# A transformer attention stage in double periods: scores of four units in one burst, two weighted sums back to back

## The reference, cut to what matters

```
x = x + L0_attn(L0_cond(x, cond), W_qkv, W_out)     # 16 heads of 64, causal
   qkv    = inputs @ W_qkv
   score  = einsum('bihd,bjhd->bijh', q, k) / 8, masked to j <= i
   w      = softmax(score, axis=2)
   out    = einsum('bijh,bjhd->bihd', w, v) @ W_out
h = L0_cond2(x)                                     # gates f, i, h:
   f, i   = sigmoid(x @ W_f + b_f), sigmoid(x @ W_i + b_i)
   f_n,i_n= f / (f + i + eps), i / (f + i + eps)
   hidden = scans over the positions of f_n and i_n * (x @ W_h + b_h)
x = x + L0_ffn(h) ; x = x + L1_attn(...) ; x = x + L1_ffn(...)
```

## Time and profile before

| | |
|---|---|
| Median of 3 runs | 1017.2 us (1015.59 to 1017.58) |
| Profiled execution, its span | 1016.5 us |
| PE busy | 977.0 us (96%) |
| PE weight loads busy | 789.2 us (78%) |
| DVE busy | 876.8 us (86%) |
| ACT busy | 831.3 us (82%) |
| POOL busy | 471.2 us (46%) |
| Scores of the first attention (L341) | first at 15.4 us, last at 422.0 us |

### The profile page before, as it was taken

How to read it: one execution, slowest core, us unless ns; L and a number is a source line. 1 busy time by engine, 2 the same in 40 slices (tenths; PEclk the granted TensorE clock), 3 DMA queues, 4 the chain that set the end, 5 groups by cost and what they waited for, 6 DMA issues and landing times.

```text
span 1016.5 us, 25956 instructions
## 1 busy us (share of the span) xinstructions
PE 977.0 (96%) x8939; PEld 789.2 (78%) x8939; DVE 876.8 (86%) x3718; ACT 831.3 (82%) x2232; POOL 471.2 (46%) x541
## 2 busy tenths in 40 slices
PE   7999999999999999999989999999999999999897
PEld 6898888888888989743268988888777777776566
DVE  6777989898989888799998899889988888896985
ACT  6888888888888888887797878776887888886786
POOL 2334545454545463606810112102887888893041
PEclk9999999999999999999999999999999999999999
DMA  9000000000000000000000000000000000000002
GB/s 376 35 2 2 2 2 2 2 2 2 2 2 2 2 2 2 2 1 0 1 1 1 1 1 1 1 11 11 23 23 23 23 23 23 23 3 1 1 2 84
DMA packets 8723, 18.31 MB, mean 18 GB/s; under 512 B 1296, under 2 KB 5648, under 8 KB 8208
## 3 DMA queue, kind: packets, MB, share of 16 engines
q1 hardware_dynamic: 8592, 16.65, 4.9%
HBM read 10.36 MB, written 2.10 MB: 12 GB/s over the span
## 4 chain that ended last, share of the span: by engine, by line
PE 79%; DVE 9%; ACT 6%; POOL 3%; issue 3%; DMA 0%; DVEq 0%; ACTq 0%; POOLq 0%
PE PB L245 8%; PE PB L246 8%; PE PB L247 8%; PE PB L341 6%; PE PB L396 6%; PE PB L379 6%; PE PB L1798 5%; PE PB L1195 3%; PE PB L1770 3%; PE PB L1197 3%; PE PB L1196 3%; PE PB L1815 3%; PE PB L428 2%; PE PB L429 1%; PE PB L430 1%
## 5 line engine op out<-in xcount | busy, mean ns | idle before, releaser
L371 POOL TENSOR_TENSOR W<-W,small 128x512 f32<-128x512 f32 x128 | 138.5, 1082 | 216.3 <-DVE small L365 216.3
L360 ACT ACTIVATE W<-W,small 128x128 f32<-128x128 f32 x512 | 198.8, 390 | 29.6 <-DVE small L351 29.0
L245 PE MATMUL PB<-RR_s 128*128 128x256 f32 (+3 forms) x568 | 184.4, 325 | 3.5 <-issue 1.9
L246 PE MATMUL PB<-RR_s 128*128 128x256 f32 (+3 forms) x568 | 176.8, 311 | 0.0
L247 PE MATMUL PB<-RR_s 128*128 128x256 f32 (+3 forms) x568 | 176.7, 311 | 0.0
L351 DVE CUSTOM_DVE_ANT_0 W<-PB,W 128x128 f32<-128x128 f32 x512 | 117.3, 284 | 39.1 <-PE PB L341 38.1
L1786 POOL TENSOR_TENSOR AR_s<-AR_s,small 128x512 f32<-128x512 f32 x128 | 129.3, 1040 | 15.9 <-DVE small L1779 15.8
L1169 ACT ACTIVATE AR_s<-PB,W 128x512 f32<-128x512 f32 (+2 forms) x160 | 100.5, 629 | 28.5 <-PE PB L247 22.1
L245 PEld LDWEIGHTS PB<-RR_s 128*128 128x128 f32 x568 | 108.6, 191 | 11.1 <-issue 4.2
L1183 DVE TENSOR_TENSOR RR_s<-AR_s,RR_s 128x512 fp32r<-128x512 f32 (+2 forms) x160 | 100.4, 636 | 17.1 <-ACT RR_s L1174 13.8
L1779 DVE CUSTOM_DVE_ANT_0 AR_s<-PB,W 128x128 f32<-128x128 f32 x512 | 111.0, 286 | 2.6 <-PE PB L1770 0.9
(11 more groups left out here) (385 smaller groups left out, 2437.0 us busy)
## 6 DMA issues: line engine op xcount, KB each, us to landing
W<-in_w SPq DMA_DIRECT2D x1, 5809.5 KB, 25.5
W<-in_w SPq DMA_DIRECT2D x2, 1024.0 KB, 7.2
out<-XT SPq DMA_DIRECT2D x8, 256.0 KB, 2.3
XF<-in_xT SPq DMA_DIRECT2D x3, 512.0 KB, 10.9
W<-AR_s SPq DMA_DIRECT2D x16, 64.0 KB, 2.1
AR_s<-AR_s SPq DMA_DIRECT2D x16, 64.0 KB, 2.1
QS<-AR_s SPq DMA_DIRECT2D x12, 64.0 KB, 2.1
KR<-AR_s SPq DMA_DIRECT2D x12, 64.0 KB, 2.1
```

Of the source, the lines that this page charges most:

```text
L245: nc.tensor.matmul(out, lh, rh, start=True, stop=False)
L246: nc.tensor.matmul(out, ll, rh, start=False, stop=False)
L360: e = nc.scalar.activation(SS[r][:, hl], SS[r][:, hl], ACTF.Exp, bias=mx[r][:, h:h + 1], scale=-1.0, accum_out=rc[r][:, h:h + 1])
L371: nc.gpsimd.tensor_tensor(s3, s3, over(rc[r], 2, [128, 4, 128]), ALU.mult).then_inc(s_nrm, 1)
```

## The change

The period of the attention becomes four units, two v: z counts 32 double periods (`NP`). TensorE does the scores of all four units first, then the four transposes of the previous double period with the projections between them, and the two weighted sums at the end. The scores of a unit pair now share banks PB0 and PB1, or PB2 and PB3. The rings of SS, mx and rc grow from 6 to 8 units, that of q and k shrinks from 3 to 2 v. `dve_max` waits for both units of its pair. ScalarE's and VectorE's lists are written anew for four units, and with them the list of banks. In the last double period, `pe_layers` and its partners are reordered too.

```diff
-        QK = [[ar(512) for _ in range(2)] for _ in range(3)]
+        QK = [[ar(512) for _ in range(2)] for _ in range(2)]
-        SS = [cs(w(x), i) for x in ("wq", "wk", "wv") for i in range(2)]
+        SS = [cs(w(x), i) for x in ("wq", "wk", "wv") for i in range(2)] + [ar(512) for _ in range(2)]
...
-        passes("v", 0, s_vp, 1)
-        for v in range(NV + 3):
-            for pr in range(2):
-                if v + 2 < NV:
-                    passes("k", 2 * v + 4 + pr, s_qk, 2 * v + 5 + pr)
-            if v + 1 < NV:
-                passes("v", v + 1, s_vp, v + 2)
-            if v % 4 == 1 and v // 4 + 1 < NCH:
-                passes("u", v // 4 + 1, s_uf, v // 4 + 2)
-            if v >= 4 and v % 2 == 0:
-                passes("y", v // 2 - 2, s_y, v // 2 - 1)
+
+        def plan_gates(v):
             for s in (2 * v, 2 * v + 1):
                 c, i = divmod(s - 22, 16)
                 if 0 <= c < 7 and i < 3:
                     passes("fih"[i], c, s_ga, 3 * c + i + 1)
-            if 0 <= v - 2 < NV:
-                passes("o", v - 2, s_ot, v - 1)
+
+        for z in range(NP):
+            if z + 1 < NP:
+                passes("k", 4 * z + 4, s_qk, 4 * z + 5)
+                passes("k", 4 * z + 5, s_qk, 4 * z + 6)
+            passes("v", 2 * z, s_vp, 2 * z + 1)
+            plan_gates(2 * z)
+            if z % 2 == 0 and z // 2 + 1 < NCH:
+                passes("u", z // 2 + 1, s_uf, z // 2 + 2)
+            if z >= 2:
+                passes("y", z - 2, s_y, z - 1)
+            if z + 1 < NP:
+                passes("k", 4 * z + 6, s_qk, 4 * z + 7)
+                passes("k", 4 * z + 7, s_qk, 4 * z + 8)
+            passes("v", 2 * z + 1, s_vp, 2 * z + 2)
+            plan_gates(2 * z + 1)
+            if z:
+                passes("o", 2 * z - 2, s_ot, 2 * z - 1)
+                passes("o", 2 * z - 1, s_ot, 2 * z)
+        passes("y", NP - 2, s_y, NP - 1)
+        passes("o", NV - 2, s_ot, NV - 1)
+        passes("o", NV - 1, s_ot, NV)
+        passes("y", NP - 1, s_y, NP)
...
-            dve.wait_ge(s_S, 2 * (v - 3) + 2)
+            dve.wait_ge(s_S, 2 * (v - 2) + 2)
...
-            return PB[2 * (u % 2) + h % 2][:, h // 2 * 128:h // 2 * 128 + 128]
+            at = u % 2 * 256 + h // 2 * 128
+            return PB[2 * (u // 2 % 2) + h % 2][:, at:at + 128]
 
         def pe_S(u):
             v, b = divmod(u, 2)
             pe.wait_ge(s_qk, 2 * v + 2)
-            pe.wait_ge(s_max, 4 * (u - 1))
+            pe.wait_ge(s_max, 8 * (u // 2 - 1))
             for h in range(4):
                 r = slice(64 * (h % 2), 64 * (h % 2) + 64)
-                qk = QK[v % 3][h // 2]
+                qk = QK[v % 2][h // 2]
                 mm = nc.tensor.matmul(score(u, h), qk[r, b * 128:b * 128 + 128], qk[r, 256 + b * 128:256 + b * 128 + 128], start=True, stop=True)
             mm.then_inc(s_S, 1)
 
         def dve_max(u):
-            r = u % 6
+            r = u % 8
             dve.wait_ge(s_wc, 16)
-            dve.wait_ge(s_T, u - 5)
-            dve.wait_ge(s_S, u + 1)
+            dve.wait_ge(s_T, u - 7)
+            dve.wait_ge(s_S, 2 * (u // 2) + 2)
...
-            pe_v(0)
-            for v in range(NV - 1):
-                for b in range(2):
-                    if v < NV:
-                        pe_S(2 * v + b)
-                if 0 <= v - 1 < NV:
-                    pe_T(2 * v - 2)
-                for b in range(2):
-                    if v + 2 < NV:
-                        pe_k(2 * v + 4 + b)
-                if v + 1 < NV:
-                    pe_v(v + 1)
-                if v % 4 == 1 and v // 4 + 1 < NCH:
-                    pe_u(v // 4 + 1)
-                if 0 <= v - 1 < NV:
-                    pe_T(2 * v - 1)
-                if v >= 4 and v % 2 == 0:
-                    pe_y(v // 2 - 2)
-                for s in (2 * v, 2 * v + 1):
-                    if gate_step(s):
-                        pe_gated(*gate_step(s))
-                if 0 <= v - 2 < NV:
-                    pe_PV(v - 2)
+            for z in range(NP - 1):
+                for u in range(4 * z, 4 * z + 4):
+                    pe_S(u)
+                if z:
+                    pe_T(4 * z - 4)
+                pe_k(4 * z + 4)
+                if z:
+                    pe_T(4 * z - 3)
+                pe_k(4 * z + 5)
+                pe_v(2 * z)
+                pe_gates(2 * z)
+                if z % 2 == 0 and z // 2 + 1 < NCH:
+                    pe_u(z // 2 + 1)
+                if z:
+                    pe_T(4 * z - 2)
+                if z >= 2:
+                    pe_y(z - 2)
+                pe_k(4 * z + 6)
+                if z:
+                    pe_T(4 * z - 1)
+                pe_k(4 * z + 7)
+                pe_v(2 * z + 1)
+                pe_gates(2 * z + 1)
+                if z:
+                    pe_PV(2 * z - 2)
+                    pe_PV(2 * z - 1)
...
-            act_vp(0)
-            for v in range(NV):
-                for s in split_steps(v):
+            for z in range(NP):
+                if z >= 2:
+                    act_oh(2 * z - 4)
+                    act_oh(2 * z - 3)
+                act_exp(4 * z)
+                if z:
+                    act_pt(4 * z - 4)
+                act_exp(4 * z + 1)
+                if z:
+                    act_pt(4 * z - 3)
+                act_vp(2 * z)
+                act_gates(2 * z)
+                if z:
+                    act_pt(4 * z - 2)
+                act_exp(4 * z + 2)
+                if z % 2 == 0 and z // 2 + 1 < NCH:
+                    act_uh(z // 2 + 1)
+                if z:
+                    act_pt(4 * z - 1)
+                for s in split_steps(2 * z + 1):
                     act_xh(*s)
-                if 0 <= v - 3 < NV:
-                    act_oh(v - 3)
-                if v < NV:
-                    act_exp(2 * v)
-                if 0 <= v - 1 < NV:
-                    act_pt(2 * v - 2)
-                if v < NV:
-                    act_exp(2 * v + 1)
-                if v % 4 == 1 and v // 4 + 1 < NCH:
-                    act_uh(v // 4 + 1)
-                if v + 1 < NV:
-                    act_vp(v + 1)
-                if 0 <= v - 1 < NV:
-                    act_pt(2 * v - 1)
-                if v in (1, 2):
-                    act_wout(v - 1)
-                if v == 4:
+                if z + 1 == NP:
+                    act_vp(2 * z + 1)
+                act_exp(4 * z + 3)
+                if z + 1 < NP:
+                    act_vp(2 * z + 1)
+                act_gates(2 * z + 1)
...
-            for v in range(NV + 1):
-                for c, hf in split_steps(v):
-                    if hf:
-                        dve_xl(c, hf)
-                if v < NV:
-                    dve_max(2 * v)
-                if 0 <= v - 3 < NV:
-                    dve_ot(v - 3)
-                if v < NV:
-                    dve_max(2 * v + 1)
-                if v + 2 < NV:
-                    dve_qk(2 * v + 4)
-                if v < NV:
-                    dve_rc(2 * v)
-                if v + 2 < NV:
-                    dve_qk(2 * v + 5)
-                if v % 4 == 1 and v // 4 + 1 < NCH:
-                    dve_uf(v // 4 + 1)
-                for step in dve_gate_steps(2 * v):
-                    dve_gated(*step)
-                if v < NV:
-                    dve_rc(2 * v + 1)
-                for c, hf in split_steps(v):
-                    if not hf:
-                        dve_xl(c, hf)
-                for step in dve_gate_steps(2 * v + 1):
-                    dve_gated(*step)
-                if v % 4 == 1 and v // 4 + 1 < NCH:
-                    dve_ul(v // 4 + 1)
-                if v in (1, 2):
-                    dve_wout(v - 1)
-                if v == 4:
+            for z in range(NP):
+                if z:
+                    dve_rc(4 * z - 1)
+                if z >= 2:
+                    dve_ot(2 * z - 4)
+                dve_max(4 * z)
+                dve_max(4 * z + 1)
+                if z >= 2:
+                    dve_ot(2 * z - 3)
+                dve_gates(4 * z)
+                dve_max(4 * z + 2)
+                if z + 1 < NP:
+                    dve_qk(4 * z + 4)
+                dve_rc(4 * z)
+                dve_max(4 * z + 3)
+                if z + 1 < NP:
+                    dve_qk(4 * z + 5)
+                dve_rc(4 * z + 1)
+                if z % 2 == 0 and z // 2 + 1 < NCH:
+                    dve_uf(z // 2 + 1)
+                dve_gates(4 * z + 1)
+                if z >= 2:
+                    dve_y(z - 2)
+                if z + 1 < NP:
+                    dve_qk(4 * z + 6)
+                if z % 2 == 0 and z // 2 + 1 < NCH:
+                    dve_ul(z // 2 + 1)
+                for s in split_steps(2 * z + 1):
+                    dve_xl(*s)
+                dve_gates(4 * z + 2)
+                if z + 1 < NP:
+                    dve_qk(4 * z + 7)
+                dve_rc(4 * z + 2)
```

(27 more changed lines are left out.)

58 lines of the change are left out of this document (39 added, 19 removed).

## The result

The changed kernel takes 1061.4 us (median of 4, 1060.4 to 1063.5) against 1017.4 for the kernel before on the same chip: ratio 1.0436, 95% interval 1.0424 to 1.0448. It is slower, by 44 us.

The account below looks back on a forecast made before the run. The prediction took TensorE's order at its own pace as the bound, VectorE close behind. Bank waits added 57 us over six gated rounds, other double periods the rest of 61: 1016.5 + 61 = 1077.5, given as 1078 us; range 1050 to 1100.

Parts of the forecast that it names:

- TensorE alone: Attention on TensorE: grouped scores and weighted sums save 0.43 us per double period, 13 us over 30.
- ScalarE: Second transposes wait 0.7 us per double period for ScalarE's copy of the first, now behind a unit's exponentials.
- VectorE, z mod 4 = 0: Double periods with z a multiple of four: TensorE's bank waits for late q/k copies make 15.5 us, not about 12.9.
- The other kinds: Other gated double periods, laid out likewise: 17.1 us for z mod 4 = 1, 15.4 for 2, 13.9 for 3.
- the double periods around them: Double periods outside the six gated rounds: z = 2 to 4 +1 us, z = 5 +0.6, z = 30 +2.7.
- the end of the stage: Start and last double period: later maxima against v's postponed projection, taken as 0, bounds -3 to +4 us.
- the split of x alone: VectorE's split of x averaged 1.0 us with GpSimd beside it, could take 0.6: 5 us in all.
- the weight loads' share: Sign in the changed profile: TensorE's weight-load busy share from 30 to 430 us falls from 89% to about 76%.
- the clock: Rival: longer TensorE gaps lower its clock, adding some 1.7 us in each of 25 gated periods: 1120 us; 7%.
- TensorE's own pace: Rival: VectorE's copies arrive in time, so TensorE keeps its pace and saves 13 us: 1004 us; 6%.
- ScalarE alone: Rival: only ScalarE's bank binds, costing 0.3 us 30 times, with VectorE's delays hidden in it: 1026 us; 6%.
- The reading by weight loads: First attention: TensorE's weight loads at 89% put VectorE, at 86%, level; the prediction used start times but called this second limit near.

Follow-up runs that it names:

- experiment 6: Changed kernel with experiment 5's edits, plus VectorE's first and second q/k copies ahead of a unit's maxima and the split of x behind the fourth copy: 1026.7 us.
- experiment 9: experiment 6 plus the gates' f and i projections and activations half a double period later and a reordered last double period: 1014.6 us, ratio 0.997.
- experiment 1: Changed kernel with only VectorE's gates' steps moved behind its copies of q and k and the output projection's addition: 1036.0 us, ratio 1.0191.
- The probe: Kernel before, preceded by VectorE scans, subtractions and reciprocals, with GpSimd idle, then beside its multiplications: four scans 1.37 and 5.48 us; total time says nothing.
- experiment 2: Changed kernel with only TensorE's second, third and fourth transposes moved to later or other places among the projections: 1095.2 us, ratio 1.077.
- 10: Kernel before, with one group of VectorE's gates' steps per half-period ahead of the second unit's maxima and both q/k copies: 1057.4 us, ratio 1.0396.
- experiment 5: Changed kernel with the edits of experiment 1 and experiment 2, plus ScalarE's third-unit exponentials ahead of its copy of the third transposes: 1044.5 us, ratio 1.027.
- experiment 7: experiment 6, with the four scans behind the fourth copy and split of x and ScalarE copying v earlier, only where z mod 4 = 1: 1032.3 us.

## Why the prediction was right, and where its size was off

The mechanism and the sign were right: 1078 forecast with 1050 to 1100 as its own range, 1061.4 measured. By its own steps:

- *TensorE alone.* 1.90 us for the two weighted sums, 1.99 for four units' scores (2.04 forecast). Of the 0.43 us per double period, three kinds of experiment 6 show 0.3 to 0.5, and experiment 9 0.2 over a whole round. The saving is there; its full size isn't shown.
- *ScalarE.* Second transposes 3.93 us after the scores forecast, 3.90 measured. The wait came 31 times, 0.6 us each. With VectorE's copies in time it is nearly all that TensorE waits for, as experiment 1 shows.
- *VectorE, z mod 4 = 0.* Forecast and measured, from the scores: first copy done 7.0 and 6.4; chunk's product 7.1 and 6.6; output projection 8.7 and 8.0; its addition begins 10.5 and 9.8; fourth copy done 14.45 and 13.3; period 15.5 and 14.39. The order of waits is the forecast one. Some 0.6 us of the 1.1 is the first group of scans, busy 1.36 us instead of 1.85; 0.35 more comes between the third and the fourth copy, where the low part of the chunk's first product (L299) and the scans gave way to the next step sooner than their busy times said; the rest is spread over the copies.
- *The other kinds.* 15.4 and 13.9 for z mod 4 = 2 and 3 came out at 15.30 and 14.02. For z mod 4 = 1, 17.1 came out at 15.28: scans 1.36 instead of 1.86, the split of x 0.42 instead of 1.0, four state steps 1.13 instead of 1.55.

The mis-sized term is therefore these three groups of VectorE steps. The two kinds were forecast 2.9 us too long per round, and some 2.2 of it are these groups, about 13 us over six rounds. The whole miss, 16.6 us, is 18.4 in the six rounds and 2.2 in the double periods around them (4.3 forecast, 2.1 measured), less the 3.9 that the end of the stage cost and that I had taken at 0. So two errors partly cancelled. I took the durations from the earlier trace rows, where GpSimd ran beside a part of these steps: in the trace of before, beside 7 of 32 scans L525, 6 of 32 scans L537, 6 of 32 state steps and 15 of 16 splits. In the changed kernel it ran beside none of the scans and state steps, and beside 6 of 16 splits. I had cited that as unknown for the split of x alone, at 5 us. The probe shows the price of a neighbour on GpSimd: about one GpSimd operation for each scan.

Also off: a projection takes 0.13 us, not 0.125 (2.36 / 18 in the earlier trace rows; the sum has 0.79 for six); the weight loads' share was to fall to 76%, it fell to 81%; scores were to end at 483 us and ended at 457: 20.6 us from the shorter double periods, and 5.4 because the last two units' scores now stand right behind the others. VectorE was to wait longer for the scores and waits less, 27.0 us instead of 37.9; for the output projection it does wait longer, 20.9 instead of 2.0. The end of the stage had -3 to +4 as bounds.

Of the rivals, the clock didn't fall in the changed kernel: 1.00 in the stage. That this was not far off is shown by experiment 2, where it fell four times. TensorE's own pace (1004) and ScalarE alone (1026) were refuted by the waits and by experiments 1 and 10. The reading by weight loads and not by busy matmuls (the Trainium skill, "Perfetto Trace Analysis", Identifying the Most-Contended Engine), that VectorE was nearly level with TensorE, fits the outcome: VectorE's order decided the time, and where the faster order on TensorE gained 3 us, VectorE is at 90% and the weight loads at 91%.

How much each layer costs is only known in this order of edits. The first gives 25 us; the rest to the kernel before, 18, and the 3 beyond it come from the copies ahead of the maxima, the split of x, the transposes' and ScalarE's order, the last double period, and the f and i gates, which were changed together or one upon another; their single shares in the changed kernel stay open.

## What to carry to other kernels

When products take their banks in turn, an elementwise engine's copies out of them are the schedule: keep steps that free nothing behind the copies, and check, for each product, the copy that stands three places before it. Moving a group on one engine means checking its counterpart on every other engine's list: the move of the transposes cost 34 us with ScalarE's list and VectorE's unchanged, and with both adapted (experiment 5) it was still 8.5 us slower than not moving them. And before steps are put off to a later place, look at the tiles that the next chunk overwrites: a step that frees no bank may free such a tile, as in experiment 7.

## What the runs showed of the hardware

In the probe, VectorE's scans and subtractions, which read two inputs from SBUF, hardly progressed beside GpSimd's multiplications: each of four scans took 1.37 us instead of 0.34 (a quarter of 5.48 and of 1.37), about the time of one GpSimd operation (1.33, an eighth of 10.63). GpSimd's first operation, before the scans began, took 1.26 us, and the median of the eight was 1.37. The reciprocals, with one input, took the same in both passes, the two beside GpSimd included. In the kernel before, the scans L525 show the same split (shortest, median and longest in ns):

```profile
L525 DVE TENSOR_TENSOR_SCAN W<-W,small x28: 391/394/1259, 118.4 to 428.9; 128x128 f32<-128x128 f32 x28
```

The 25 of all 32 with no GpSimd operation beside them took 0.395 us, the 7 others 0.95; the mean from 100 to 300 us was 0.52. In the changed kernel none had one, and the mean was 0.40. The repaired orders bring the neighbour back: the scans L551 take 0.67 us in the mean from 30 to 440 us of experiment 1, against 0.40 in the changed kernel. The Trainium skill, "SBUF — State Buffer", Terms, has the rule for this: VectorE and GpSimd share a pair of ports, locked for a whole instruction, and the loser blocks fully. The probe agrees, with the numbers above.
